# Last steps of a fused attention and sparse network kernel: who splits tile 30's masked activations, and where its second layer stands

## The reference, cut to what matters

```python
z = xn @ ternary_quant(W_syn).T + b_syn              # 512 -> 2048
thresh = top_k(z, 204)[-1]                           # per row
hidden = where(z >= thresh, relu(z), 0)              # about 10% is kept
out = hidden @ ternary_quant(W_out).T + b_out        # 2048 -> 512
ffn = layernorm(xn + out, gamma, beta)
# attention: 16 heads of 32, chunks of 128 rows with a decaying state carried from chunk to chunk,
# a mask of decay factors instead of softmax, an RMS norm of the result, then @ Wo
```

## Time and profile before

| what | value |
| --- | --- |
| median of 3 runs | 953.33 us (952.49 to 953.53) |
| the profiled execution's own time | 952.98 us |
| its span, first to last instruction | 951.2 us |
| PE busy | 904.9 us (95%) |
| DVE, ACT busy | 732.2 us, 730.3 us (77% each) |
| POOL busy | 659.0 us (69%) |
| mean granted TensorE clock | 0.984 of full speed |

### The profile page before, as it was taken

The page is one execution under the profiler, slowest core; times in us unless marked ns, Lnnn a source line. Parts: engine busy times, 40 slices in busy tenths (PEclk is TensorE's granted clock), DMA queues, the critical chain, the costliest instruction groups (busy, mean ns, idle before and its releaser), DMA issues.

```text
span 951.2 us, 22133 instructions
## 1 busy us (share of the span) xinstructions
PE 904.9 (95%) x8307; PEld 443.2 (47%) x8307; DVE 732.2 (77%) x1826; ACT 730.3 (77%) x1322; POOL 659.0 (69%) x588
## 2 busy tenths in 40 slices
PE   4857999999999999999999999999999999999987
PEld 2423544444444444444444444444444444444434
DVE  5869877877777787777778777777787777778775
ACT  6788778887777887777778887777887777779672
POOL 1535688677677767767876776877766767886763
PEclk9977999999999999999999999999999999999999
DMA  9875644444444354543534444444354444444431
GB/s 336 242 199 100 119 81 76 91 100 79 87 93 99 69 91 89 95 85 79 101 80 77 90 101 79 85 95 94 64 98 92 90 87 82 90 84 85 79 66 47
DMA packets 257422, 94.49 MB, mean 99 GB/s; under 512 B 243488, under 2 KB 243744, under 8 KB 256544
## 3 DMA queue, kind: packets, MB, share of 16 engines
q1 hardware_dynamic: 253472, 85.64, 45.4%
q10 hardware_dynamic: 3840, 7.41, 2.2%
HBM read 24.34 MB, written 8.39 MB: 34 GB/s over the span
## 4 chain that ended last, share of the span: by engine, by line
PE 77%; ACT 7%; issue 6%; DVE 3%; DMA 3%; POOL 2%; SPq 1%; DVEq 1%; ACTq 0%; POOLq 0%
PE proj L1108 42%; PE p_ffn L1220 10%; PE p_wo L1267 8%; PE p_ffn L1250 8%; PE rows L1176 3%; PE rows L1166 2%; ACT Pr L647 2%; ACT hl L665 1%; DMA area<-in_L_ffn_W_syn_dram 1%; PE rows L1187 1%; PE rows L1197 1%; DMA area<-in_L_attn_Wk_dram 1%; SPq L275 1%; DVE c L1656 1%; PE p_ffn L1236 1%
## 5 line engine op out<-in xcount | busy, mean ns | idle before, releaser
L1108 PE MATMUL proj<-wqkv,xT 128*128 128x512 f16 x1152 | 261.2, 384 | 1.9 <-ACT area L489 0.7
L1108 PE MATMUL proj<-wsynT,xT 128*128 128x512 f16 x1024 | 246.8, 385 | 5.3 <-DMA wsynT<-xrn 4.0
L907 POOL TENSOR_TENSOR hl<-area,hl 128x2048 f16<-128x2048 f32 x31 | 141.2, 4556 | 98.0 <-ACT hl L665 98.0
L1108 PEld LDWEIGHTS proj<-wqkv,xT 128*128 128x128 f16 x1152 | 111.9, 99 | 135.2 <-ACT area L489 10.9
L1108 PEld LDWEIGHTS proj<-wsynT,xT 128*128 128x128 f16 x1024 | 93.6, 99 | 118.5 <-issue 11.9
L1510 DVE SCALAR_TENSOR_TENSOR area<-proj,c,gb 128x512 f32<-128x512 f32 x128 | 95.4, 746 | 38.4 <-PE proj L1108 36.4
L1220 PE MATMUL p_ffn<-woutT,area 128*128 128x512 f16 x480 | 109.3, 378 | 0.0
L1250 PE MATMUL p_ffn<-woutT,area 128*128 128x512 f16 x480 | 108.7, 379 | 0.0
L1606 DVE MAX8 cand<-area 128x8 f32<-128x128 f32 x512 | 105.2, 277 | 1.1
L1267 PE MATMUL p_wo<-wo,ahl 128*128 128x512 f16 x384 | 90.3, 384 | 1.2 <-ACT ahl L467 0.7
L1682 DVE SCALAR_TENSOR_TENSOR area<-area,c 128x2048 f32<-128x2048 f32 x32 | 75.2, 2350 | 18.7 <-ACT c L552 18.3
(11 more groups left out here) (251 smaller groups left out, 1733.4 us busy)
## 6 DMA issues: line engine op xcount, KB each, us to landing
xrn<-in_L_attn_x_dram SPq DMA_DIRECT2D x32, 256.0 KB, 3.1
out_dram<-pair_b SPq DMA_DIRECT2D x29, 256.0 KB, 2.0
woutT<-in_L_ffn_W_syn_dram ACTq DMA_DIRECT2D x2, 1024.0 KB, 11.1
area<-in_L_ffn_W_syn_dram ACTq DMA_DIRECT2D x2, 1024.0 KB, 11.9
woutT<-in_L_ffn_W_out_dram SPq DMA_DIRECT2D x2, 1024.0 KB, 6.3
area<-in_L_attn_Wq_dram ACTq DMA_DIRECT2D x1, 1024.0 KB, 6.8
area<-in_L_attn_Wk_dram ACTq DMA_DIRECT2D x1, 1024.0 KB, 9.7
area<-in_L_attn_Wv_dram ACTq DMA_DIRECT2D x1, 1024.0 KB, 11.8
```

The source lines that it names most:

```text
L907: nc.gpsimd.tensor_tensor(hl[:, 1, :], src, hl[:, 0, :], ALU.subtract).then_inc(S["lo_ready"], 1)
L1108: last = nc.tensor.matmul(bank, xT[:, b.par, k, :], w, start=m == 0, stop=m == len(pairs) - 1)
```

## The change

GpSimd copies T30's masked activations to float16 (a `tensor_scalar` that multiplies by 1 twice), ahead of everything else that it does in its last steps; `out_scaled(T28)` and `out_added(T28)` go behind `q_joined(T31)` and `attention_low(T30)`. The difference is made by VectorE between `attention_normalised(T30)` and `below(T31)`. ScalarE drops its copy and fills `p_ffn` ahead of `attention_high(T30)`. TensorE runs `network_high(T30)` inside `attention_projected(T30)`, ahead of its four low matmuls, then T31's values, then `network_low(T30)`; `squares_summed(T31)`, `factors_spread(T31)` and `last_failures` follow it.

```diff
@@ ScalarE, last_steps
                 guess_settled(T31)
+                network_seeded(T30)
                 attention_high(T30)
-                hidden_high(T30, z[:, 0, :])
                 third_count(T31)
                 out_stats(T29)
-                network_seeded(T30)
                 attention_out(T31)
@@ GpSimd, last_steps
                 wait(pool, "h_ready", T30, 1, 1)
+                wait(pool, "hiT", T30, 16, 0)
+                nc.gpsimd.tensor_scalar(hl[:, 0, :], z[:, 0, :], 1.0, 1.0, ALU.mult, ALU.mult).then_inc(S["hi_ready"], 1)
+                q_joined(T31)
+                attention_low(T30)
                 out_scaled(T28)
                 out_added(T28)
-                q_joined(T31)
-                attention_low(T30)
-                hidden_low(T30, z[:, 0, :])
                 out_root(T29)
@@ TensorE, last_steps
                 scores(T31)
-                attention_projected(T30)
+                attention_projected(T30, lambda: network_high(T30))
                 earlier_values(T31)
                 values(T31)
-                network_high(T30, lambda: squares_summed(T31), 11)
+                network_low(T30)
+                squares_summed(T31)
+                last_sums()
                 last_failures()
-                network_low(T30, last_sums)
                 attention_projected(T31, lambda: last_flipped(0))
@@ VectorE
+            def last_difference():
+
+                wait(dve, "hi_ready", T30, 1, 1)
+                wait(dve, "loT", T30, 16, 0)
+                nc.vector.tensor_tensor(hl[:, 1, :], z[:, 0, :], hl[:, 0, :], ALU.subtract).then_inc(S["lo_ready"], 1)
@@ VectorE, last_steps
                 attention_normalised(T30)
+                last_difference()
                 below(T31)
```

## The result

The changed kernel takes 966.57 us (median of 4 runs, 965.9 to 967.14), the one before 953.28 us in the same runs: ratio 1.0134, 95% interval 1.0118 to 1.0149. It is slower, by 13.3 us or 1.3%. The forecast was 965.6 us.

What follows compares the result with a forecast made beforehand. TensorE bounds regular steps (95% busy); in the last 40 us a chain across engines does. Span 951.2 + 10.9 (later T31 start) + 1.7 (second clock fall) = 963.8, stated as 965.6 us measured; range 961.5 to 968.5.

Steps and rivals of the forecast that it cites:

- (f): TensorE's tail: the clock falls again before the final 11.5 us of work, eight matmuls at half clock, 1.7 us more.
- (b): VectorE's new difference for T30: 2.3 us, so below(T31) runs 1.0 us later.
- (e): TensorE: T31's values wait for the late transpose until 929.9, clock falls; T31's attention_projected starts at 944.8, 10.9 us later.
- (d): GpSimd's and SyncE's order: T28's store waits until 924.6 and holds T30's transposes; the high half lands at 929.85.
- (a): GpSimd's float16 copy of T30: 2.0 us, hi_ready at 915.5.
- rival 3: GpSimd's copy costs 4.1 us and more, everything behind it comes 1.8 us later: 967.5 us; chance 0.17.
- (c): ScalarE: network_seeded ahead of attention_high(T30) delays that copy and TensorE's first eight matmuls 0.6 us, at no cost.
- rival 1: TensorE's delay as forecast, but the clock does not fall again in the tail: 964.2 us; chance 0.25.
- Rival 2: T30's transpose is not held by SyncE's store: 952.9 us with the clock up, 954.2 with it down; chance 0.05.

Runs made afterwards that it cites:

- The first experiment: The changed kernel, but SyncE issues both transposes of T30 ahead of the store of T28: 953.89 us, ratio 0.9999 to the kernel before.
- the fastest kernel: The changed kernel with SyncE's transposes ahead of T28's store, squares_summed(T31) inside network_low(T30) and unread matmuls in the tail: 951.87 us, ratio 0.9980 to the kernel before.
- the last experiment: The fastest kernel plus five unread matmuls on either side of scores(T31), with q_joined(T31) ahead of GpSimd's wait for masked activations: 951.85 us, ratio 0.9983.

## Why the prediction was right

From GpSimd's start on T30 to T31's L1267 it was 933.90 - 913.46 = 20.44 us before and 945.38 - 913.01 = 32.37 us after: 11.93 later, where the sum had 10.9. The tail behind it grew by 18.92 - 17.3 = 1.62, where (f) had 1.7. With the 0.45 us that this execution was ahead, the span grew by 11.93 + 1.62 - 0.45 = 13.1. So the mechanism was right, and the 1 us that is missing lies in (b) and (e).

- **(d), the held transposes.** Shown: the store at 924.70 (924.6 was forecast), the transpose 0.44 us behind it, TensorE going on at 929.82 (929.9). That these times agree to 0.1 us is partly luck: counted from the mark the store was 0.55 us and the landing 0.37 us later than forecast, and the 0.45 us by which this execution was ahead hides that. With the order on SyncE alone changed, the loss goes. It is the cause.
- **(a), the copy.** 1.90 us (2.0). The high end, rival 3, is out. That the landing weighs is shown by the copy on ScalarE.
- **(b), the difference.** 2.85 us (2.3). The duration itself was right, 2.29 us where it runs alone; what I did not count is GpSimd's `q_joined` at 914.87 to 916.02 beside it. The store came 0.5 us later by it.
- **(c).** The first eight matmuls started 0.6 us later, as forecast, and it cost nothing, as the next ones waited for the DMA.
- **(e).** The mis-sized term: I had 5.2 us for the 16 matmuls behind the gap, eight of them slow; from the first to the next row it was 935.84 - 929.82 = 6.0. The slow stretch is not of one length: 8 matmuls at 1.2 GHz took from 3.2 to 3.6 us in the tail, and 5.3, 5.8, 6.07 and 6.18 us were measured for the 16.
- **(f), the second fall.** Shown in the profile after (3.52 us for eight matmuls), and rival 1, which left it out, had 964.2. Matmuls in the gap alone take it away in one profile (the tail filled, the squares behind `network_low`). The profiles of all runs fall into groups: with `squares_summed` behind `network_low` and nothing added the fall is there in five of five; with the squares inside the second layer of T30 (the kernel before, TensorE's old order, the squares inside `network_low`) it is absent in three of three; with matmuls added in the tail it is absent in four of four. That is one execution each, and why the place of the squares would decide it is not shown.
- **Rival 2**, the transpose not held, had 954.2 and, with the clock up, 952.9. The first experiment is this case: 953.89. Its own working left out that the second fall would stay. In the profile the first fall was absent, so T31's L1267 came 0.22 us sooner than in the kernel before (0.45 was forecast for the clock up, 0.85 later for the clock down), but the tail was 1.68 us longer. The profiled execution is thus about 1.5 us behind the profiled one of the kernel before, from the same mark, while the medians are equal; one profile each does not say how often either fall comes. That the time is so near to the rival's numbers is partly luck.

What stays open: the sum of both clock terms in one execution, and how the 0.2% of the fastest kernel splits between the squares' place and the filled tail; the first alone was not told apart from nothing, the second, on top of it, was worth 1.4 us.

## What to carry to other kernels

When an operation is moved later, look for every engine that waits for its result, a DMA issuer above all, and read what that issuer has queued behind the wait: here a store that nobody needed held a transfer that everybody needed, and swapping them was worth some 13 us (ratio 1.0134 against 0.9999). Moving TensorE work ahead of a critical step pays only if its operand is sure to be there, for a late one holds up the step and lets the clock fall besides. Where small matmuls alternate with waits ahead of a burst, matmuls that nobody reads can keep the burst at full speed.

## What the runs showed of the hardware

- GpSimd and VectorE, with two operands in SBUF each, take turns by whole instructions: 1.27 and 1.15 us became 3.20 and 3.19 us on GpSimd, and 2.34 became 3.36 and 2.29 became 2.85 on VectorE. The one that had started first went on, and the other waited until its end; the one exception is the last experiment, where the starts are 0.01 us apart and GpSimd's, the later one, went first. Beside VectorE's L1584, which takes one of its two large operands from TensorE's output banks, GpSimd's L937 in the profile after kept its 1.27 us. The Trainium skill, SBUF — State Buffer, section "Who interferes with whom", has it that a VectorE instruction with two SBUF inputs contends with a GpSimd instruction that reads SBUF, for a port pair under an exclusive lock; the rows agree. The 1.54 us of L912 in the earlier trace rows, 1.16 elsewhere, fit it too, as it started beside VectorE's `q_decayed`.
- GpSimd's one-operand copy from float32 to float16 took 1.90 us for 128x2048, less than the 1.99 us of L893 in the earlier trace rows.
- The granted clock can fall after TensorE has restarted: behind 2.43 us of idleness it was at 1.00 when the matmuls began at 929.89 and at 0.5 from 930.5 on.
- Between executions the fall in front of L1267 for T30 comes and goes, with the same list on TensorE up to there and the same waits ahead (1.33 and 1.35 us): 3.25 to 3.43 us for eight matmuls in four of nine profiles, the changed kernel's among them, and 1.90 in the other five, that of the first experiment among them.
